# Both seams of a graph network's node pass: the first pair is loaded in the stage before, and the wait for the last stores moves to the stage behind

## The reference

```python
x = ln(x + gen(x))   # softmax aggregation over edges, then W1, norm, relu, W2; contains + x
x = ln(x + gin(x))   # sum over edges, w1, relu, w2, batch norm over nodes, relu; contains + x
x = ln(x + cf(x))    # weights from 20 edge features, sum over edges, softplus update
x = ln(x + sage(x))  # mean over edges, W1l/W1r, relu, mean over edges, W2l/W2r
```

## Time and profile before

| | |
|---|---|
| median of 3 runs | 2331.14 us (2329.19 to 2331.57) |
| the profiled execution, its own time | 2333.73 us |
| span of the profile, first to last instruction | 2332.0 us |
| busy: PE, DVE, ACT, POOL | 89%, 85%, 76%, 55% of the span |
| mean granted TensorE clock | 0.955 of full speed |
| `edges_first` | 1101.13 to 1301.95 us |
| `nodes_alone` | 1303.13 to 1694.66 us (last store issued) |
| `edges_middle` | from 1698.33 us |

### The profile page before, as it was taken

How to read it: one execution, slowest core, us unless ns; L and a number is a source line. 1 busy time by engine, 2 the same in 40 slices (tenths; PEclk the granted TensorE clock), 3 DMA queues, 4 the chain that set the end, 5 groups by cost and what they waited for, 6 DMA issues and landing times. The chain is left out here.

```text
span 2332.0 us, 45639 instructions
## 1 busy us (share of the span) xinstructions
PE 2076.6 (89%) x14017; PEld 1727.5 (74%) x14017; DVE 1993.2 (85%) x2947; ACT 1780.6 (76%) x3691; POOL 1275.3 (55%) x1115
## 2 busy tenths in 40 slices
PE   5999999999999799998999688999889999688563
PEld 4999999999999577776677577777657776566553
DVE  7999999999999566666899599999879999699664
ACT  4989889999988477776777488999879998576321
POOL 5766655665640323331386488830037776578676
PEclk9999999999999899999899799999989999799886
DMA  4656565555565788886798589875537778577751
GB/s 114 164 161 160 147 162 161 170 155 165 176 192 166 196 251 252 252 256 192 207 220 198 119 190 204 196 183 163 161 105 215 213 211 232 142 211 200 227 176 62
DMA packets 256985, 427.17 MB, mean 183 GB/s; under 512 B 50849, under 2 KB 103252, under 8 KB 256746
## 3 DMA queue, kind: packets, MB, share of 16 engines
q1 hardware_dynamic: 210028, 367.21, 53.5%
q0 software_dynamic: 46400, 56.69, 13.0%
q10 hardware_dynamic: 318, 0.36, 0.0%
HBM read 240.16 MB, written 186.37 MB: 183 GB/s over the span
## 5 line engine op out<-in xcount | busy, mean ns | idle before, releaser
L523 PE MATMUL banks<-mats,g_hT 128*125 128x256 f32 x1000 | 259.3, 382 | 0.0
L542 PE MATMUL banks<-mats,g_zT 128*125 128x128 f32 x2000 | 238.8, 273 | 0.0
L542 PEld LDWEIGHTS banks<-mats,g_zT 128*125 128x125 f32 x2000 | 228.2, 188 | 0.0
L1857 POOL DMA_INDIRECT acc<-combined,first_ x100 | 175.6, 1756 | 73.3 <-ACT combined L1756 39.2
L1924 POOL DMA_INDIRECT em_y<-acc,from_ x100 | 103.4, 1034 | 197.7 <-PE banks L2066 167.8
L523 PEld LDWEIGHTS banks<-mats,g_hT 128*125 128x125 f32 x1000 | 189.6, 190 | 28.1 <-issue 0.4
L868 POOL DMA_INDIRECT gin_xs<-x,from_ x100 | 98.7, 987 | 186.8 <-DMA x_of_src<-gin_xs 161.9
L1043 DVE TENSOR_TENSOR gin_acc<-gin_acc,gin_qr 125x512 f32<-125x512 f32 x125 | 86.6, 693 | 119.3 <-ACT gin_qr L1003 119.3
L603 ACT ACTIVATE g_zT<-banks,cols 128x500 f32<-128x500 f32 x250 | 179.2, 777 | 2.4 <-PE banks L531 2.4
L445 POOL DMA_INDIRECT g_xd<-in_x,idx x100 | 100.1, 1001 | 143.3 <-PE banks L557 118.9
L586 ACT ACTIVATE g_sq<-banks 125x512 f32<-125x512 f32 x250 | 144.2, 591 | 38.5 <-PE banks L523 36.1
(11 more groups left out here) (420 smaller groups left out, 6546.2 us busy)
## 6 DMA issues: line engine op xcount, KB each, us to landing
acc<-g_zero SPq DMA_DIRECT2D x126, 224.0 KB
x<-g_x SPq DMA_DIRECT2D x125, 224.0 KB
g_x<-in_xT SPq DMA_DIRECT2D x100, 250.0 KB
h<-gin_hr SPq DMA_DIRECT2D x50, 448.0 KB
al_h<-h SPq DMA_DIRECT2D x38, 448.0 KB
al_x<-x SPq DMA_DIRECT2D x38, 448.0 KB
out<-al_out SPq DMA_DIRECT2D x38, 448.0 KB
gin_x<-x SPq DMA_DIRECT2D x37, 448.0 KB
```

Source lines behind the costliest of these rows:

```text
L523: m = nc.tensor.matmul(bank[0:P, 256 * j:256 * j + 256], HT[q % 2][:, c:c + P], K.W1c, start=False, stop=j == 1)
L542: m = nc.tensor.matmul(pO[q % 2][0:P, D * j:D * j + D], ZT[q % 2][:, h, P * j:P * j + P], K.W2[:, h, :], start=False, stop=j == R - 1 and ...
L1857: pool.indirect_dma_start(out=K.acc, out_offset=bass.IndirectOffsetOnAxis(ap=K.first_all[:, g, r:r + 1], axis=0), in_=CR_all[:, g, r * D:r ...
```

## The change

A new object `Head` is made before `edges_first`. It has a fixed place in SBUF for the first pair of x and of h, and the semaphores `al_xin` (three) and `al_stored` (three), which now outlive a stage. `Head.load` is called by SyncE in step 25 of `edges_first`, behind `keep(22)` and ahead of `keep(23)`. `Nodes` takes these two buffers as `X[0]` and `H[0]`, has two more of each of its own, and starts loading at pair 1. `all_stored` leaves the end of SyncE's stream in `nodes_alone`. In `edges_middle` the same wait stands on GpSimd ahead of its first scatter into the result, on ScalarE ahead of the first absolute value (`size(0)`, L2178) and on VectorE ahead of the first maximum (`positive(0)`, L2254). The semaphores are cleared one stage later than they were.

```diff
--- before.py
+++ after.py
@@ -1258,7 +1258,7 @@
 class Nodes:
 
 
-    def __init__(self, nc, K, out, name, ctx, first, count, banks, outs=3, given=None):
+    def __init__(self, nc, K, out, name, ctx, first, count, banks, outs=3, given=None, head=None):
         def sb(n, shape, dt=F32, k=2):
             return [ctx.enter_context(nc.sbuf_tensor(f"{name}_{n}{i}", shape, dt)) for i in range(k)]
 
@@ -1269,15 +1269,16 @@
         self.pH, self.pA, self.pX, self.pU, self.pC = banks
         self.outs = outs
         if given is None:
-            self.X, self.H, self.OUT = [sb(n, [P, 2 * R, D], k=k) for n, k in (("x", 3), ("h", 3), ("out", outs))]
+            self.X, self.H, self.OUT = [[None] * (3 - k) + sb(n, [P, 2 * R, D], k=k) for n, k in (("x", 2), ("h", 2), ("out", outs))]
             self.A, self.B = sb("a", [P, 2 * R, D]), sb("b", [P, 2 * R, D])
-            self.loaded = 0
+            self.X[0], self.H[0] = head.x, head.h
+            self.loaded = 1
         else:
             self.X, self.H, self.OUT, self.A, self.B = given.X, given.H, given.OUT, given.A, given.B
             self.loaded = 2
         self.BT, self.XT, self.HT = sb("bT", [128, G]), sb("x3T", [128, G]), sb("h3T", [128, G])
         self.na, self.nb, self.nc_ = [Pairs(nc, K, f"{name}_{n}", ctx) for n in ("na", "nb", "nc")]
-        self.xin, self.stored = given.xin if given else sem_list(K, f"{name}_xin", 3), sem_list(K, f"{name}_stored", outs)
+        self.xin, self.stored = (given or head).xin, sem_list(K, f"{name}_stored", outs) if given else head.stored
         (self.hT, self.bt, self.back, self.a, self.x2, self.b, self.x3, self.x3T, self.xt, self.u, self.ht, self.cs, self.done) = [
             sem(n) for n in ("hT", "bt", "back", "a", "x2", "b", "x3", "x3T", "xt", "u", "ht", "cs", "done")]
         self.freed = self.done
@@ -1543,7 +1544,9 @@
 
     ctx = ExitStack()
     with ctx:
-        n = Nodes(nc, K, out, "al", ctx, 0, count, (K.ps[0], K.ps[1:3], K.ps[3:5], K.ps[5], K.pairs[3]))
+        n = Nodes(nc, K, out, "al", ctx, 0, count, (K.ps[0], K.ps[1:3], K.ps[3:5], K.ps[5], K.pairs[3]), head=K.head)
+        K.taken += K.head.xin
+        K.head.stored_by = n
 
         turned = Turned(nc, K, n, CR_all, got_h, 12)
 
@@ -1558,7 +1561,6 @@
                         n.store(sp, i - 4)
                     if i == count:
                         ahead(sp)
-                n.all_stored(sp)
 
             @block.tensor
             def _(pe):
@@ -1574,6 +1576,19 @@
                 steps(count, [(1, on(n.apply_a, dve)), (1, on(n.add_alone, dve)), (3, on(n.apply_c, dve)), (0, on(n.residual, dve, 0)),
                               (1, on(n.reduce_b, dve)), (0, on(n.residual, dve, 1)), (1, on(n.apply_b, dve)), (0, on(n.reduce_a, dve)),
                               (2, on(n.reduce_c, dve))])
+
+
+class Head:
+
+
+    def __init__(self, nc, K):
+        self.K = K
+        self.x, self.h = [nc.alloc_sbuf_tensor_at(f"al_first_{n}", [P, 2 * R, D], F32, offset=217632 + 4096 * i) for i, n in enumerate("xh")]
+        self.xin, self.stored = K.lasting("al_xin", 3), K.lasting("al_stored", 3)
+
+    def load(self, sp):
+        move(sp, halves(self.h), pair_of(self.K.h, 0), self.xin[0])
+        move(sp, halves(self.x), pair_of(self.K.x1, 0), self.xin[0])
 
 
 def edges_first(nc, K, CR_all, rounds, got_h):
@@ -1648,6 +1663,8 @@
                         load(i)
                     if i >= 3:
                         keep(i - 3)
+                    if i == EG:
+                        K.head.load(sp)
                 for i in range(3):
                     sp.wait_ge(kept[i], 32 * ((EG - i + 2) // 3))
 
@@ -1989,7 +2006,8 @@
 
         X, Y, XD, YD = ins.X, ins.Y, ins.XD, ins.YD
         xin, din, got, IV = ins.xin, ins.din, ins.got, ins.IV
-        K.taken += xin + din + got
+        K.taken += xin + din + got + K.head.stored
+        rows_stored = K.head.stored_by.all_stored
         YT, YTD = sb("yT", [128, G]), sb("ydT", [128, G])
         A, B, BD, C = sb("a", [P, R, D]), sb("b", [P, R, D], k=3), sb("bd", [P, R, D], k=3), ins.slot
         AB, SP, ABD, SPD = sb("ab", [128, G]), sb("sp", [128, G]), sb("abd", [128, G]), sb("spd", [128, G])
@@ -2014,6 +2032,8 @@
                         ins.get(pool, k)
 
                 def put(k):
+                    if k == 0:
+                        rows_stored(pool)
                     if k < EG - 1:
                         past(pool, done, k)
                         ends.put(pool, k)
@@ -2175,6 +2195,8 @@
                 def size(k):
                     past(act, o1, k)
                     past(act, sp_, k - 2)
+                    if k == 0:
+                        rows_stored(act)
                     nc.scalar.activation(AB[k % 2][:, :], pG[:, 0:G], ACT.Abs, bias=K.c("bo1")).then_inc(ab, 1)
 
                 def expo(k):
@@ -2251,6 +2273,8 @@
                 def positive(k):
                     past(dve, ab, k)
                     past(dve, upd, k - 2)
+                    if k == 0:
+                        rows_stored(dve)
                     nc.vector.tensor_scalar(SP[k % 2][:, :], pG[:, 0:G], K.c("bo1"), 0.0, ALU.add, ALU.max).then_inc(rl, 1)
 
                 def soft(k):
@@ -2510,6 +2534,7 @@
         CR_all = big.enter_context(nc.sbuf_tensor("combined", [128, EG, R * D], F32))
         ROUNDS, PAIRS = 10, NG // 2 - LATE
         got_h = K.lasting("h_got", 4)
+        K.head = Head(nc, K)
         edges_first(nc, K, CR_all, ROUNDS, got_h)
         K.end_phase()
         inputs = ExitStack()
```

## The result

| | before | after |
|---|---|---|
| median (lowest to highest) | 2331.14 us (2323.07 to 2334.43), 7 runs | 2318.35 us (2313.22 to 2321.86), 7 runs |
| ratio of after to before | | 0.9946, 95% interval 0.9933 to 0.9959 |
| profiled execution, span | 2333.73, 2332.0 | 2315.6, 2313.8 |

The change takes off 0.54% (0.41 to 0.67%), 12.6 us by the ratio.

A forecast was written before the change was run, and what follows sets the result against it. No engine is full over the span: seven stages in a row with barriers, the node stage running on VectorE. 6.2 + 2.3 - 0.1 = 8.4 us off the median 2331.14 gives 2322.7 us; range 2319.5 to 2325.5.

The forecast's parts named there:

- First seam, 6.2 us: Start of node stage: first pair loaded early brings the first activation from 7.51 to 1.30 us in; 6.2 us gained.
- Second pair, cost zero: Node stage start: second pair's transposes wait 0.2 us for their bytes, taken up by 2.4 us of slack; cost zero.
- The table load: Node stage start: the skill's 2.66 us switch rule would give 4.85 us in place of 6.2; the sum does not use it.
- Second seam, 2.3 us: Node stage's end: SyncE no longer waits for its stores' landing, so 3.67 us becomes 1.33; 2.34 us go.
- Waits added, 0.1 us: Middle edge stage: semaphore waits added on ScalarE, VectorE and GpSimd are already met; cost 0 to 0.3 us, taken as 0.1.
- The middle stage as long as before: Middle edge stage, behind the second seam: expected to keep its length, no gain or loss there.
- The noise term: Whole run: half the spread of three runs, 1.2 us, allowed in the bounds of the likeliest outcome.
- The low bound of the likeliest case: Whole run: likeliest 2321.5 to 2324.2 us, from bounds 6.17 to 6.21, 2.3 to 2.5, 0 to 0.3, and 1.2 us.
- A: Node stage's filling: TensorE keeps 2.4 GHz, 2.1 us less on the path; gain 10.5, 2320.6 us; chance 0.12.
- B: Node stage's end: barrier holds SyncE until its stores land, so that seam gives nothing; 2325.0 us; chance 0.05.
- C: Node stage's end: seam gets dearer by 3.5 us with stores in flight; gain 2.6, 2328.5 us; chance 0.06.
- D: Node pass: VectorE's residual reads moved tiles more slowly; at a third more than 678 ns, 2339.9 us; chance 0.03.

The follow-up runs named there:

- late_gathers: Kernel after plus five extra GpSimd gathers near the node stage's end, into a free tile, rows used nowhere; median 2320.67 us (1 run).
- after_spin: Kernel after plus 8 and 10 extra TensorE products in each of the node stage's first two pairs; 2316.73 us, ratio 0.9943 against the kernel before.

## Why the prediction was right in kind and too small

**First seam, 6.2 us: mechanism right, size about 1 us low by the means.** The first activation stands at 1.30 us in all nine profiles with the edit, as read from the last edge stage. Without it the first transposes waited for their bytes until 6.4, 7.5, 7.3 and 6.7 us in; the one execution that I had was the lowest, and in the mean 6.9 us fall away. The filling behind them has no fixed length in either kernel. By node stages: 391.5, 389.1, 391.4 and 388.4 us without the edit (mean 390.1), with it five of 381.6 to 381.7 and two of 385.2 (mean 382.7). The difference of the means, 7.4 us, is the best figure for the term, with some 2 us of doubt either way (an estimate from the scatter of these stages), so 6.2 is low but not shown to be wrong; the 9.8 of the first two profiles is a long one against a short one. The length goes with when the clock first falls: from 1 to 2 us into the stage it is 1.00 in the two long ones and 0.79 to 0.94 in the five short ones. Why it falls sooner or later is open.

**Second pair, cost zero: right.** It waited 1.51 us in place of 0.2, under the slack of 2.4.

**The table load: right.** The Trainium skill, "ScalarE: Activation LUTs", section "What ACT_TABLE_LOAD costs", gives 2.66 us for "every switch to a different set", which would have put the first activation there; the trace has it at 1.29, 0.01 us behind the load. All stages of this kernel load one and the same set (`natural_log_exp_and_others`), so no run here shows a switch, and the page and the trace need not differ: the prediction held the rule against a case that it does not name.

**Second seam, 2.3 us: right.** 3.67 to 3.70 us without the edit, 1.29 with it: 2.4.

**Waits added, 0.1 us: not seen.** ScalarE's first absolute value stands 5.66 us into the middle stage after and 5.67 before, VectorE's first maximum 6.37 and 6.38.

**"The middle stage as long as before": wrong, and this is the step that failed.** Without the second edit it takes 320.5, 320.9, 321.0 and 321.8 us (mean 321.0), with it, and without products behind the node pass, 319.1, 319.8, 319.4, 319.1, 319.5 and 319.6 (mean 319.4): 1.6 us less in the mean, and the two groups do not meet. TensorE stands 6.3 us ahead of it in place of 8.6, and full clock is back 11 to 12 us into it in place of 16 to 17. I asked what the edit does to the seam, and not what it does to the filling behind it. The length of the standing isn't the whole rule: in late_gathers TensorE stood 10.6 us, and the clock was back at 11.

Together 7.4 + 2.4 + 1.6 = 11.4 us. The three timings of the whole change gave 12.6, 9.3 and 13.0 us by their ratios, mean 11.6. The medians of the result lie 12.8 us apart, 4.4 more than the 8.4 forecast. About 3.0 of these are in the terms: 1.6 of the middle stage, 1.2 of the first seam, 0.2 of the other two. The other 1.4 us are the draw of this timing.

**The noise term, "half the spread of the three runs, 1.2 us": wrong.** Over 29 runs the kernel before spread from 2320.16 to 2336.47 us, and layer 2, which nobody touched, took 323.3 to 327.7. With half the range of layer 2 alone, 2.2 us, in the place of 1.2 the low end would be 2318.5, 0.15 us above the result. The low bound of the likeliest case is also mis-added: 2331.14 - 6.21 - 2.5 - 1.2 is 2321.2, not 2321.5. And the gap before the next store is 6.9 us, not 6.5, which changes nothing.

**The rivals.** A as told is out: the first transposes ran at the full clock (0.62 us in place of 1.09), but it is 0.51 in 1300 to 1302 and the second set took 1.06 us, the slow value. What it rests on is real, though: the filling's clock is worth 3 us (after_spin). B is out by the 1.29 us, C by the same, though late_gathers shows that such a price exists; D by the residual's 677 ns.

## What to carry to other kernels

A seam is priced with the filling behind it: what is gained or lost there includes how soon TensorE's clock comes back, so read the granted clock of the first 30 us of each stage, and try a few spare products where TensorE stands just before a stage or in its filling, so few that they end before the barrier or the data they precede. Here they shortened the stages by 3 us each; by whole times the gain over the kernel after is not shown. A landing time, a filling and a run's noise are drawn anew in each execution; a term read from one profile, or a bound from three runs, needs a margin of the size that untouched stages show. Keep indirect transfers of GpSimd away from the last microseconds before a barrier.

## What was not expected of the hardware

- A barrier of all engines took 1.19 us at the first seam, 1.29 with SyncE's stores in flight at the second, and 5.57 us when GpSimd had issued five gathers in the 8 us up to SyncE's last issue.
- TensorE at 1.2 GHz in the filling of the node pass cost 2.9 us of the path, and at the start of the middle stage 3.1 us (319.5 against 316.4); 20 products of 0.23 us each, whose results nothing reads, gave the latter back (36 did too, but held up the barrier by 2.8 us).
- The same code filled its pipeline in 32.1 or in 34.8 us, and the clock's record tells which: 13.6 or 20.5 us of it low. Layer 2, which no edit touches, took 323.3 to 324.0 us with 9 to 13 us of low clock in it and 325.7 to 327.7 with 16 to 24.
